# First attention: the rounded high part of the probabilities taken by a second exponential from the scores' PSUM bank

## What is computed

```
scores = einsum('bhqd,bhkd->bhqk', q, k_h) / sqrt(16)
scores = where(causal, finfo.min, scores)
attn = softmax(scores)
ctx = einsum('bhqk,bhkd->bhqd', attn, v_h)
x = x + ctx @ Wo
```

## Time and profile before

| | |
|---|---|
| median of 3 runs | 1508.34 us (1506.69 to 1511.98) |
| the profiled execution, its own time | 1508.7 us |
| its span, first to last instruction | 1506.9 us |
| mean granted clock of PE | 0.975 of full |
| busy over the span | PE 92%, DVE 68%, ACT 47%, POOL 46% |
| L1480, exponentials | 160, 92.4 us busy, 587 ns each |
| L1489, high parts | 160, 99.7 us busy, 629 ns each |
| L1571, low parts | 160, 203.8 us busy, 1289 ns each |

### The profile page before, as it was taken

How to read it: one execution, slowest core, us unless ns; L and a number is a source line. 1 busy time by engine, 2 the same in 40 slices (tenths; PEclk the granted TensorE clock), 3 DMA queues, 4 the chain that set the end, 5 groups by cost and what they waited for, 6 DMA issues and landing times. The chain is left out here.

```text
span 1506.9 us, 20239 instructions
## 1 busy us (share of the span) xinstructions
PE 1393.5 (92%) x7032; PEld 1076.9 (71%) x7032; DVE 1020.9 (68%) x1925; ACT 712.5 (47%) x1550; POOL 686.8 (46%) x529
## 2 busy tenths in 40 slices
PE   4779999996599789999999999999999999699999
PEld 3656666664355568888888888888888887578887
DVE  6768997784745667777677777787677777532323
ACT  3458886673322245445444544445444454343332
POOL 3458886683432444344244442444335431045543
PEclk9989999998699999999999999999999999999999
DMA  2000000000300201011010110101101001033332
GB/s 104 22 7 2 1 1 1 1 1 24 90 1 0 70 15 43 14 29 42 15 31 27 29 38 13 36 28 29 36 10 41 22 8 36 7 91 99 91 99 79
DMA packets 63808, 50.22 MB, mean 33 GB/s; under 512 B 7638, under 2 KB 53078, under 8 KB 63452
## 3 DMA queue, kind: packets, MB, share of 16 engines
q1 hardware_dynamic: 63708, 48.94, 11.1%
HBM read 46.83 MB, written 2.10 MB: 32 GB/s over the span
## 5 line engine op out<-in xcount | busy, mean ns | idle before, releaser
L1571 POOL TENSOR_TENSOR a_p_lo<-a_prob,a_p_hi 128x512 fp32r<-128x512 f32 x160 | 203.8, 1289 | 78.6 <-ACT a_p_hi L1489 76.3
L681 ACT ACTIVATE a_pt_hi<-a_ring 128x512 fp32r<-128x512 f32 x160 | 93.8, 596 | 178.6 <-PE a_ring L391 178.4
L817 POOL TENSOR_TENSOR a_rot_a<-a_rot_a,a_rot_b 128x512 f32<-128x512 f32 x80 | 103.3, 1292 | 146.8 <-DVE a_rot_b L560 145.9
L672 ACT ACTIVATE a_prob<-a_score,a_nmax 128x128 f32<-128x128 f32 (+3 forms) x256 | 131.9, 528 | 57.8 <-DVE a_nmax L525 57.7
L332 PE MATMUL a_xo<-h_hi,a_w_hi 128*128 128x512 f32 x384 | 153.9, 401 | 5.3 <-POOL a_w_lo L827 4.2
L2098 POOL TENSOR_TENSOR f_w_lo<-raw,f_w_hi 128x512 fp32r<-128x512 f32 (+2 forms) x66 | 90.5, 1396 | 145.2 <-ACT f_w_hi L2041 145.2
L334 PE MATMUL a_xo<-h_hi,a_w_lo 128*128 128x512 f32 x384 | 151.3, 394 | 0.0
L333 PE MATMUL a_xo<-h_lo,a_w_hi 128*128 128x512 f32 x384 | 150.1, 391 | 0.0
L822 POOL TENSOR_TENSOR a_p_lo<-a_rot_a,a_p_hi 128x512 fp32r<-128x512 f32 x80 | 103.7, 1296 | 72.7 <-ACT a_p_hi L698 72.7
L542 DVE TENSOR_TENSOR a_pt_lo<-a_ring,a_pt_hi 128x512 fp32r<-128x512 f32 x160 | 108.5, 687 | 33.8 <-ACT a_pt_hi L681 32.6
L525 DVE TENSOR_REDUCE a_nmax<-a_score 128x1 f32<-128x384 f32 (+3 forms) x176 | 109.3, 636 | 17.2 <-PE a_score L381 12.2
(11 more groups left out here) (276 smaller groups left out, 3768.4 us busy)
## 6 DMA issues: line engine op xcount, KB each, us to landing
raw<-in_L_gate_up_t SPq DMA_DIRECT2D x40, 256.0 KB, 3.0
raw<-in_L_attn_wq SPq DMA_DIRECT2D x32, 256.0 KB, 2.8
raw<-in_L_attn_wo SPq DMA_DIRECT2D x32, 256.0 KB, 2.6
raw<-in_L_down_t SPq DMA_DIRECT2D x20, 256.0 KB, 2.7
x<-in_L_attn_x SPq DMA_DIRECT2D x4, 512.0 KB, 5.6
raw<-in_L_attn_wk SPq DMA_DIRECT2D x8, 256.0 KB, 2.8
raw<-in_L_attn_wv SPq DMA_DIRECT2D x8, 256.0 KB, 2.8
out<-x SPq DMA_DIRECT2D x8, 256.0 KB, 2.5
```

The lines of the kernel that those rows point to most:

```text
L672: nc.scalar.activation(prob[i % 2][:, h, 0:n], score[e % NS][:, (h % per) * n:(h % per + 1) * n], ACT.Exp, bias=nmax[:, i % 2, h:h + 1], a ...
L817: nc.gpsimd.tensor_tensor(rot_a[:, c % 2, :], rot_a[:, c % 2, :], rot_b[:, c % 2, :], ALU.add).then_inc(summed, 1)
L1571: nc.gpsimd.tensor_tensor(p_lo[:, mm % NP, :], prob[:, mm % NE, :], p_hi[:, mm % NP, :].bitcast(F32), ALU.subtract).then_inc(p_ready, 1)
```

## The change

The high part is no longer a rounding copy of `prob`. ACT takes the exponential of the bank a second time, now with `F32R` as output type, into `p_hi`. So `high` needs nothing of its own tile's first exponential any more, and the semaphore `exped` is gone. The bank, however, has a second reader, and PE's wait before it writes tile mm is now for `high` of tile mm-2 instead of the exponential of tile mm-2. The lists of all engines stay as they are.

```diff
@@ turned_scores (PE)
                 if mm >= 2:
-                    pe.wait_ge(exped, mm - 1)
+                    pe.wait_ge(p_hi_done, mm - 1)
@@ exponentials (ACT)
-                nc.scalar.activation(prob[:, mm % NE, :], turned[mm % 2][:, :], ACT.Exp).then_inc(exped, 1)
+                nc.scalar.activation(prob[:, mm % NE, :], turned[mm % 2][:, :], ACT.Exp)
@@ high (ACT)
                 mm = weight_at(u, i, x, j)
-                act.wait_ge(exped, mm + 1)
                 if mm >= NP:
                     act.wait_ge(weighed, mm - NP + 1)
-                nc.scalar.activation(p_hi[:, mm % NP, :], prob[:, mm % NE, :], ACT.Copy).then_inc(p_hi_done, 1)
+                nc.scalar.activation(p_hi[:, mm % NP, :], turned[mm % 2][:, :], ACT.Exp).then_inc(p_hi_done, 1)
```

More of the change, by code:

```diff
@@ L1072, in attend0 @@
             "keys_read", "qm_read", "score_read", "parted", "c_read", "divided", "head_ready", "c_ready"))
-        q_read, exped, p_hi_done, p_ready, wo_hi_done, wo_ready, c_hi_done = (sem(n) for n in (
-            "q_read", "exped", "p_hi_done", "p_ready", "wo_hi_done", "wo_ready", "c_hi_done"))
+        q_read, p_hi_done, p_ready, wo_hi_done, wo_ready, c_hi_done = (sem(n) for n in (
+            "q_read", "p_hi_done", "p_ready", "wo_hi_done", "wo_ready", "c_hi_done"))
         block = ctx.enter_context(nc.Block())
```

## The result

The changed kernel took 1545.9 us (median), against 1508.3 for the kernel before: 37.6 us more, ratio 1.0248 (95% interval 1.0221 to 1.0275). This is the median of three executions; a fourth, at a mean granted clock of 0.651, took 2033.7 us and is left out. Forecast were 1533.5 with a range of 1516 to 1549: the sign and the mechanism held, the size was a third too small (25 us).

A forecast was written before the change was run, and what follows sets the result against it. PE was taken to bound the first attention. Shortfalls of 40.1 us in units 2 to 8 times 0.55 gave 22, plus 3 for the first unit: +25 us on 1508.3, forecast 1533.5, range 1516 to 1549.

The forecast's parts named there:

- The bound and the place: First attention: PE is the bound and waits for ACT's high part, some 25 us, at tiles 0, 11 or 12, 14, 16.
- What is removed: ACT's high part takes 0.59 us and loses its own exponential's wait, ending up to 0.17 us earlier.
- Tiles 0, 11, 12, 14, 16: Third unit: PE's writes come later behind high parts, by 0.63, 0.54, 0.68 (after 0.3 given back), 0.70 and 0.95 us.
- the 0.3 taken as given back to DVE: Third unit, after tile 11: turns where PE already waits for DVE absorb 0.3 us of its delay.
- Tiles 9 and 10: small ones ... I keep 0.1: Third unit: tile 9's delay is given back where PE waits 0.27 us for DVE anyway; 0.1 us kept.
- Tiles 15, 17, 18: +0: Third unit: these tiles are already due late enough through PE's delay, so they add 0 us.
- The walk: Tile-by-tile pass through the third unit with the new durations, giving 3.3 us of PE delay.
- The share of 0.55: 3.3 of the third unit's 6.0 us are paid; applied to the 40.1 us of units 2 to 8, giving 22.
- the shortfalls: First attention: 81 of 160 tiles were written before the high part of tile mm-2 ended, by 50.2 us in all.
- The last sum: Whole kernel: the +25 us set against the median of 1508.3 us, given as 1533.5 us.
- No overlap: Rival: DVE or POOL fall back behind PE and shortfalls add in full, +50 us, 1558 us; chance 0.08.
- The clock: Rival: PE stops more often and its granted clock falls, +39 us, 1547 us; chance 0.06.

The follow-up runs named there:

- half subtraction: POOL's subtraction on 256 of 512 columns from the fifth tile on: 1532.3 us in the changed kernel, 1498.0 us in the kernel before.

## Why the prediction was right, and where it was too small

- **The bound and the place: right.** PE was the bound, the loss is in `attend0`, at full clock in the steady part, most of it as PE's wait for `a_p_hi`, and the four places named (0, 11 or 12, 14, 16) all show a step.
- **What is removed: right.** The high part lasts 597 ns (0.59 forecast), and ACT's freedom from its own wait is worth 2 us by itself. In the changed kernel, where the high part is on PE's path, its earlier end gives back up to 7.
- **Tiles 0, 11, 12, 14, 16: right to 0.14 us** (0.63, 0.54, 0.38, 0.70, 0.95 against 0.67, 0.57, 0.35, 0.71, 1.09). At 12 both parts held: the 0.3 taken as given back to DVE was 0.38, and the stop behind the high part, 0.68 forecast, was 0.73.
- **"Tiles 9 and 10: small ones ... I keep 0.1": the step that failed most.** Together with tile 7 they cost 1.57 us, and nothing came back at the turn after tile 9, where PE's wait for DVE grew from 0.27 to 1.13. I took DVE as fixed in time and its waits as slack; but DVE follows PE's scores, and its short instructions ran into POOL's in the new timing. The trace of before told it, and I passed over it: L1336, 8 columns wide, takes 0.18 us in the median and up to 1.19. Where exactly POOL's and DVE's instructions would meet in the new timing could hardly have been forecast. L1385 ahead of tile 7 starts at 170.94, 0.05 us before one of POOL's subtractions ends and as the next begins, stands behind both and lasts 1.45 us; before, it lasted 0.29.
- **"Tiles 15, 17, 18: +0": failed at 17** (0.60 with 15 and 18). The walk moved the high parts but not the copy of queries ahead of one of them.
- **The share of 0.55: a consequence.** In units 2 to 5 and in the last the loss is 0.9 to 1.0 of the shortfalls. In units 6 and 7 it is 0.5; why is not shown. In the first unit it is 5.8 and not 3. (The last sum has a slip without weight: 1508.3 + 25 is 1533.3.)
- **The rivals.** "No overlap" (+50, chance 0.08) came near the truth in the steady units, but by luck: in the third unit shortfalls do vanish (0.58 at tile 15 is a step of 0.07), and what DVE adds at tiles 7 and 10 makes up for them. The clock was a small part at the most. It is 1.00 in the steady windows. In the first unit it is 0.96 where it was 1.00, in the last 0.87 where it was 0.90; if all of that time were lost it would be 1.6 us (0.04 x 39.3) and 2.4 us (0.13 x 63.4 - 0.10 x 58.1), of 38.4.

The Trainium skill's sentence on consistent bubbles ("Perfetto Trace Analysis", section "Optimization Strategy") held in the end: the gap repeated in each unit, and a third bank removed it, though at the price of another ring's.

What stays open is a full account of what the half subtraction brings the kernel before. In its third unit the gain stands at tiles 10 and 12 (0.35 and 0.31 us), in its last unit 1.6 of 4.15 us at tile 10, where PE had waited 1.5 us for DVE's L1336. The rest of the last unit's gain and the 1.6 us of the first are not explained. Nor is it shown why the change costs more, and not less, at half width in the last three units.

## What to carry to other kernels

Before a second reader is put on a double buffer, list for each buffer when the new last reader ends and when the producer in fact reused it before: each reuse that came sooner is a stop of the producer, and where the producer is the bound most of them may be paid (here 38 of 50 us, a part of it by way of other engines). In the walk, move every instruction of the in-order queue that stands ahead of a mover, and treat no engine's waits as slack before its own releaser is known. If the buffer cannot be had, the ring behind it and the order of the queue take back some of the loss (here 23 of 38 us); the changed kernel stayed slower than the one before.

## What the runs showed of the hardware

DVE's L1385, L1334 and L1336, which have all operands in SBUF, stand still while POOL's subtraction runs. In the kernel before 43 of these 96 started during one, and each ended 0.03 to 0.16 us behind it. In the changed kernel 48 did. Of these 43 ended 0.03 to 0.17 us behind it; the other 5, all L1385, had started in its last 0.06 us, as POOL's next one began (at most 0.03 us later). Each stood behind that one too and ended 0.15 us behind it, after some 1.45 us. Of the 32 L1385 in the changed kernel 18 lasted over twice the shortest. Those that read a PSUM bank, L1377, L1378, L1380, L1358 and L1367, never varied by more than 0.02 us. The Trainium skill ("SBUF — State Buffer", section "Terms") says that DVE and GpSimd arbitrate for one shared pair of ports by an exclusive lock, held for the full instruction, and the trace agrees: 0.17 us becomes 1.19 beside a subtraction of 1.28 us.

An ACT exponential and a copy of 128x512 last the same from SBUF (629 and 631 ns); the exponential from PSUM lasts 0.03 to 0.04 us less (597 and 588).
